# Two padded tail keys taken out of the probability-times-value products of a cross-attention and state-space kernel

## The chip, the cores and the metric

The kernel runs on one core of one Trainium2 chip. The metric is the device time of one execution in microseconds (us), as the median of several runs. PE is TensorE, PEld its weight loads, DVE is VectorE, ACT is ScalarE, POOL is GpSimd and SP is SyncE, whose queue issues DMAs.

## The reference, cut to what matters

```python
x  = layernorm(builder_state, g1, beta1)         # 4096 tokens x 512
bn = layernorm(base_state, g1, beta1)            # 3202 context rows x 512
q, k, v = heads(x Wq), heads(bn Wk), heads(bn Wv)  # 8 heads of 64
attn = softmax(q k^T / sqrt(64))                 # 4096 x 3202 for each head
x  = residual + (attn v) Wo + bo
U  = (layernorm(x, g2, beta2) W_in + b_in) Bmat
s_t = silu(s_{t-1} A^T) + U_t                    # 4096 steps
out = x + s Cmat + mean(program_probs) W_prog + b_prog
```

All of it is in 32-bit floats. 3202 keys are 25 tiles of 128 and two keys more: the 26th tile holds two real keys and 126 padded ones.

## The kernel before

**Stages.** A projection stage goes through 29 groups of 256 rows, 16 of x (giving q) and 13 of the context (giving k and v). For a context group `n = 16 + g` PE does `project_v(n, 0)`, `project_k(n, 0)`, `project_k(n, 1)`, one product for a row maximum, then `project_v(n, 1)`, `project_k(n, 2)`, `project_k(n, 3)` and a second such product. ACT takes the high part of each k chunk out of PSUM (`high_k`, L646), DVE the low part (`low_k`, L911). Then comes attention in 32 units (4 head pairs times 8 blocks of 512 queries), and then a closing stage: output projection, second layernorm, the scan over tokens, the sum.

**A unit of attention.** Unit u goes through 26 key tiles in 13 steps j, two tiles a step. In each step PE does, in this order: one product for a maximum of the unit ahead (L1176, or L1181 for the tail of the keys), the scores of both tiles (a broadcast product of the shift, L1270, and three products, L1278, L1280, L1282, for a high and low split), the second product for a maximum, and `pv` (L1303) for the two tiles of the step before; the `pv` of two tiles shows as x8, four records a tile. So `pv` of tiles 24 and 25 of unit u-1 stands in step 0 of unit u. From unit 1 on, the odd tile's shift isn't a product but is added by DVE (`add_shift`, L995). ACT takes the exponential of each tile into one of six `pt` slots (`exp_tile`, L715, and L712 for tile 25, with a bias that makes the padded keys zero). DVE reduces each product for a maximum (`take_max`, L922 or L925), and the pair of PSUM banks that it frees is the only one: `maxima` waits on PE until all maxima before it are taken (`max_taken`).

**The maxima** of a unit are 26: 24 over 512 keys each (m = 0 to 23) and two over the last 130 keys (m = 24 and 25), which are shorter. The maxima of unit 0 are made in the projection stage, two in each group, and the last four behind it. Those of unit w > 0 are made 4 steps ahead and into unit w-1; unit 0 has 34 of them in its 13 steps, so that some steps have three. In later units m = 24 and 25 fall in step 8. Then `row_max` folds them, PE turns the result with four transposes (`turn_max`, L1190, in step 9) and ACT writes the shift row `sh` (`shift`, L689), which the first scores of the next unit wait for.

**The softmax sum** is taken tile by tile: tiles 1, 5, ..., 21, 24 by accumulating DMAs into `acca` (`send_a`), tiles 3, ..., 19 into `accb` (`send_b`), the other 14, tile 25 among them, by GpSimd into `accp` (`add_tile`, L533). A `pt` slot is free for the exponential six tiles later when its sum and its `pv` are done. `spread_sum` in step 3 adds over partitions, `take_den` (ACT, step 4), `fold_den` (SP), `invert` (DVE, step 6) and `spread_rden` (SP) give a broadcast of 1/sum; GpSimd multiplies O by it in tile 18 (`scale_o`, L569), ACT and GpSimd split the result, and SP stores it (`store_o`).

**The queue of SP** in unit u: wait for the scores of unit u-1, load ql, qh, in units 8 to 11 and 16 to 19 a quarter of the next keys (832 KB), then `fold_den(u-1)`, `spread_rden(u-1)`, `spread_shift(u+1)`, `store_o(u-1)`.

Of the kernel before, what the change touches and what calls it, by code (L numbers as in the profile page):

```python
# [5 lines left out]
F32 = mybir.dt.float32  # L6
# [6 lines left out]
P = 128  # L13
# [28 lines left out]
PAD_SCORE = -2.0 ** 100  # L42
# [6 lines left out]
M_FIRST = NM + 2 * M_LEAD  # L49


def maxima_of(u, j):

    if u == 0:
        first, last = M_FIRST * j // NJ, M_FIRST * (j + 1) // NJ
    else:
        first = M_FIRST + 2 * (NJ * (u - 1) + j)
        last = first + 2
    return [(i // NM + 1, i % NM) for i in range(first, min(last, NM * (UNITS - 1)))]


def turn_step(u):

    return NJ - M_LEAD if u else NM * NJ // M_FIRST + 1

# [6 lines left out]
P_TILES = [t for t in range(NT) if t not in A_TILES + B_TILES]  # L72
# [20 lines left out]
MOD_LO = 96  # L93

# [24 lines left out]
def unit(w):  # L119

    return w % BLOCKS, PAIR_ORDER[w // BLOCKS]

# [21 lines left out]
def build(nc, x, ctx, ctxb, w_qkv_t, w_o_t, w_in, bmat, w_prog_t, a_t, cmat, cols, bo_rows, b_prog, out):  # L144
    es = ExitStack()
    with es:
# [10 lines left out]
        k_scratch = nc.dram_tensor("k_scratch", [2, P, 2, KPAD], F32).ap()  # L157
        m_scratch = nc.dram_tensor("m_scratch", [2, 2, QB], F32).ap()
# [38 lines left out]
        den8 = at("den8", [P, 8], 2560)  # L197
        rden8 = at("rden8", [P, 8], 2568)
# [5 lines left out]
        mxp = at("mxp", [P, QT, HD + 1], RR + 11776)  # L204
        mx_part = at("mx_part", [P, QT, 2, 7], RR + 12040)
        oraw = at("oraw", [P, QB], RR + 12096)
        lnb = at("lnb", [P, 64], RR + 12096)
# [22 lines left out]
        pad = small[:, 31:32]  # L230
# [67 lines left out]
        max_turned = sem("max_turned"); shift_ready = sem("shift_ready")  # L298
# [32 lines left out]
        def _(sp):  # L331
# [21 lines left out]
            def store_k(g):  # L353
                for p in (0, 1):
                    sp.wait_ge(k_ready, FC * g + (p + 1))
                    keys = slice(g * GW, (g + 1) * GW)
                    sp.dma_start(k_scratch[p][:, :, keys], kk[:, p, :, keys].bitcast(F32)).then_inc(k_stored, 16)

            def spread_shift(w):
                sp.wait_ge(shift_ready, w + 1)  # L360
                sp.dma_start(m_scratch[w % 2], sh[w % 2][0:HD + 1:HD, :].bitcast(F32)).then_inc(sh_stored, 16)
                sp.wait_ge(sh_stored, 16 * w)
# [3 lines left out]
            def fold_den(u):  # L366
                sp.wait_ge(den_taken, u + 1)
                for i in range(4):
                    sp.dma_start(den8[32 * i:32 * (i + 1), :],
                                 den_sb[32 * i:32 * i + 1, 0:QB // 2].rearrange("o (p j) -> o p j", j=8)).then_inc(den8_loaded, 16)  # L370

            def spread_rden(u):
                sp.wait_ge(rden_ready, u + 1)
                sp.dma_start(r_scratch[u % 2].rearrange("h (p j) -> (h p) j", j=8), rden8[:, :]).then_inc(rden_stored, 16)
# [25 lines left out]
            for n in range(X_SLOTS, NG):  # L400
# [3 lines left out]
                if n == X_SLOTS + X_G + 1:  # L404
                    for half in (0, 1):
                        sp.wait_ge(q_stored[half], 32 * (X_G // 2))
                    load_qh(0)
                if n - X_SLOTS - 1 >= X_G:
# [3 lines left out]
            sp.wait_ge(proj_done, projected(NG - 1))  # L412
# [3 lines left out]
            store_k(C_G - 1)  # L416

# [15 lines left out]
            for u in range(UNITS):  # L433
# [30 lines left out]
            for d in range(2, X_G):  # L464
                if d >= OG_SLOTS:
# [28 lines left out]
        def _(pool):  # L494
# [5 lines left out]
            nc.gpsimd.memset(mxp[:, :, :], 0.0)  # L500
            nc.gpsimd.memset(pad[:, :], PAD_SCORE)
            nc.gpsimd.memset(ones_row[:, :].bitcast(F32), 0.0).then_inc(ones_set, 1)
            pool.wait_ge(ones_set, 1)
            nc.gpsimd.memset(pad[0:KEYS - (NT - 1) * P, :], 0.0)
# [15 lines left out]
            pool.wait_ge(proj_done, projected(NG - 1))  # L520
# [44 lines left out]

            def scale_o(u):
                pool.wait_ge(rdenb_loaded, 32 * (u + 1))
                pool.wait_ge(o_taken, u + 1)
# [12 lines left out]
            for u in range(UNITS):  # L581
                for t in range(NT):
# [4 lines left out]
                    else:  # L587
                        add_tile(u, t)
                    if t == 18 and u > 0:
# [9 lines left out]
            for d in range(2, X_G):  # L599
                add_bias(d)  # L600
                if d == 10:
# [892 lines left out]
```

## Time and profile before

| what | value |
|---|---|
| median of 3 runs | 2315.91 us (2312.77 to 2317.89) |
| the profiled execution, its own time | 2315.49 us |
| its span, first to last instruction | 2313.7 us |
| mean granted TensorE clock | 0.989 |
| PE, PEld, DVE busy | 2254.5, 1306.4, 1733.4 us |
| ACT, POOL busy | 1110.4, 1583.7 us |
| accumulating DMAs' queue (q0), other queue (q1) | 46.2% and 19.3% of 16 engines |

A row of a group gives the source line, engine, operation, output and input, shapes and count, then busy time and the mean of one. A row of the timeline gives start, length, engine, line and what ended the idle time before it. The ends of matmuls are modelled, so the start of one instruction and the start of the next tell more than the lengths.

### The profile page before, as it was taken

The numbers are of one execution on the slowest core, as the hardware profiler recorded it, in microseconds if no ns is written. First come the engines' busy times: TensorE is split into PE (matmuls) and PEld (weight loads), VectorE is DVE, ScalarE is ACT, GpSimd is POOL, SyncE is SP. The second block draws the span as 40 slices with busy tenths as digits, with TensorE's granted clock in tenths as the row PEclk, the third lists the DMA queues.
The fourth block names the chain that finished last, engine by engine and source line by source line (L and its number), as shares of the span: only waits on it lengthen the run. The fifth ranks groups of instructions, "written<-read, shape, count | busy, mean of one in ns | idle before, by whom it ended". The sixth has DMA issues, their size and how long they took to land.

```text
span 2313.7 us, 36253 instructions
## 1 busy us (share of the span) xinstructions
PE 2254.5 (97%) x14262; PEld 1306.4 (56%) x14262; DVE 1733.4 (75%) x2167; ACT 1110.4 (48%) x1422; POOL 1583.7 (68%) x1039
## 2 busy tenths in 40 slices
PE   8999989999999999999999999999999999999987
PEld 8998854554555544555555455555555555445764
DVE  5765446888888778888888788888888888755865
ACT  3654424445445445444454544544544545453454
POOL 1200026888888888888888888888888888887312
PEclk8999999999999999999999999999999999999998
DMA  6660225677777777777777777677677776787723
GB/s 241 211 193 10 83 64 118 147 160 159 157 160 155 165 167 171 174 158 161 157 159 169 174 174 173 156 166 158 151 158 162 161 160 155 185 186 172 240 100 145
DMA packets 159703, 365.02 MB, mean 158 GB/s; under 512 B 23535, under 2 KB 63087, under 8 KB 158894
## 3 DMA queue, kind: packets, MB, share of 16 engines
q0 software_dynamic: 59904, 218.13, 46.2%
q1 hardware_dynamic: 99630, 144.59, 19.3%
q8 instruction: 112, 1.84, 0.3%
q14 instruction: 57, 0.47, 0.1%
HBM read 95.41 MB, written 49.02 MB: 62 GB/s over the span
## 4 chain that ended last, share of the span: by engine, by line
PE 81%; DMA 5%; POOL 4%; issue 4%; DVE 4%; ACT 1%; POOLq 0%; SPq 0%; DVEq 0%; ACTq 0%
PE ps L1303 28%; PE ps L1176 10%; PE ps L1278 7%; PE ps L1280 7%; PE ps L1282 7%; DMA acca<-pt 5%; PE ps L1140 4%; PE ps L1270 4%; PE ps L1158 3%; PE ps L1148 3%; POOL accp L533 3%; PE ps L1368 2%; PE ps L1121 1%; DVE mx_part L922 1%; PE ps L1425 1%
## 5 line engine op out<-in xcount | busy, mean ns | idle before, releaser
L715 ACT ACTIVATE pt<-ps 128x1024 f32<-128x1024 f32 x800 | 779.3, 1021 | 908.5 <-PE ps L1282 878.2
L922 DVE TENSOR_REDUCE mx_part<-ps 128x2 f32<-128x1024 f32 x768 | 938.0, 1221 | 338.5 <-PE ps L1176 338.4
L533 POOL TENSOR_TENSOR accp<-accp,pt 128x1024 f32<-128x1024 f32 x416 | 1040.5, 2501 | 220.7 <-ACT pt L715 219.0
L1303 PE MATMUL ps<-pt,v 128*64 128x512 f32 x3328 | 805.6, 605 | 0.0
L995 DVE TENSOR_TENSOR ps<-ps,shb 128x1024 f32<-128x1024 f32 x403 | 493.1, 1224 | 52.1 <-PE ps L1282 52.1
L1303 PEld LDWEIGHTS ps<-pt,v 128*64 128x64 f32 x3328 | 201.8, 136 | 344.0 <-issue 335.3
L1176 PE MATMUL ps<-kk,qh 64*128 64x512 f32 x1536 | 349.0, 450 | 10.0 <-DVE mx_part L922 10.0
L1176 PEld LDWEIGHTS ps<-kk,qh 64*128 64x128 f32 x1536 | 143.3, 183 | 355.2 <-DVE mx_part L922 268.6
L1278 PE MATMUL ps<-qh,kk 64*128 64x512 f32 x1664 | 328.8, 391 | 6.9 <-ACT pt L715 6.9
L1280 PE MATMUL ps<-qh,kk 64*128 64x512 f32 x1664 | 328.5, 390 | 0.0
L1282 PE MATMUL ps<-ql,kk 64*128 64x512 f32 x1664 | 328.2, 389 | 0.0
L543 POOL DMA_DIRECT2D acca<-pt x192 | 183.5, 956 | 4.6 <-DMA acca<-pt 2.3
L1278 PEld LDWEIGHTS ps<-qh,kk 64*128 64x128 f32 x1664 | 157.3, 185 | 43.8 <-ACT pt L715 10.4
L1280 PEld LDWEIGHTS ps<-qh,kk 64*128 64x128 f32 x1664 | 157.1, 184 | 35.4
L1282 PEld LDWEIGHTS ps<-ql,kk 64*128 64x128 f32 x1664 | 157.3, 184 | 34.8
L1270 PE MATMUL ps<-sh,ones_row 64*128 64x512 f32 x858 | 173.8, 402 | 1.0 <-ACT pt L715 1.0
L553 POOL DMA_DIRECT2D accb<-pt x128 | 129.6, 1012 | 0.0
L522 POOL MEMSET sh<- 128x512 f32 x2 | 1.0, 530 | 187.2 <-PE ps L1158 187.2
L1368 PE MATMUL ps<-wo_hl,og 128*128 128x512 f32 x384 | 95.5, 404 | 7.0 <-DVE x_first L1038 6.1
L1270 PEld LDWEIGHTS ps<-sh,ones_row 64*128 64x128 f32 x858 | 82.4, 187 | 15.1 <-ACT pt L715 12.0
L1368 PEld LDWEIGHTS ps<-wo_hl,og 128*128 128x128 f32 x384 | 72.6, 193 | 27.4 <-issue 12.7
L578 POOL TENSOR_TENSOR xb<-xb,bo 128x512 f32<-128x512 f32 x32 | 40.7, 1326 | 65.4 <-DMA xb<-x 65.3
(154 smaller groups left out, 1898.3 us busy)
## 6 DMA issues: line engine op xcount, KB each, us to landing
acca<-pt POOLq DMA_DIRECT2D x224, 512.0 KB, 4.9
accb<-pt POOLq DMA_DIRECT2D x160, 512.0 KB, 4.8
q_scratch<-kk SPq DMA_DIRECT2D x32, 512.0 KB, 4.4
acca<-accp POOLq DMA_DIRECT2D x32, 512.0 KB, 4.6
o_scratch<-ost SPq DMA_DIRECT2D x32, 512.0 KB, 3.0
og<-o_scratch SPq DMA_DIRECT2D x32, 512.0 KB, 5.9
shb<-m_scratch SPq DMA_DIRECT2D x31, 512.0 KB, 4.1
xs<-x SPq DMA_DIRECT2D x16, 512.0 KB, 6.4
```

The source lines that it names most:

```text
L533: nc.gpsimd.tensor_tensor(acc[:, :], acc[:, :], pt[n % PT_SLOTS][:, :], ALU.add).then_inc(added_p, 1)
L543: nc.gpsimd.dma_start(acc[:, :], pt[n % PT_SLOTS][:, :], accum_op=ALU.add).then_inc(added_a[u % 2], 16)
L715: nc.scalar.activation(pt[n % PT_SLOTS][:, :], src, ACT.Exp, scale=SCALE).then_inc(exped, 1)
L922: nc.vector.tensor_reduce(mx_part[:, m % QT, :, m // QT], src, AX_X, ALU.max).then_inc(max_taken, 1)
L995: nc.vector.tensor_tensor(ps[:, b:b + 2, :], ps[:, b:b + 2, :], shb[u % 2][:, :, :], ALU.add)\
L1176: ins = mm(ps[:, bank, :], q[r, (m % QT) * P:(m % QT + 1) * P], kk[r, p, 0, a:a + QB], start=True, stop=True)
L1270: ins = mm(ps[:, 2 * (t % 2) + h, :], ones_row[r, :], sh[u % 2][r, :], start=first, stop=not first)
L1278: mm(ps[:, b + h, :], kk[r, p, 0, key], qh[u % 3][r, :], start=first, stop=False)
L1280: mm(ps[:, b + h, :], kk[r, p, 1, key], qh[u % 3][r, :], start=False, stop=False)
L1282: ins = mm(ps[:, b + h, :], kk[r, p, 0, key], ql[u % 2][r, :], start=False, stop=last)
L1303: ins = mm(ps[HD * h:HD * (h + 1), 6, :], v[:, t, f:f + HD], pt[n % PT_SLOTS][:, h * QB:(h + 1) * QB], start=(t == 0), stop=(t == NT - 1))
L1368: ins = mm(ps[:, 2 + t, :], og[:, d % OG_SLOTS, a, k, rows], wo_hl[:, b, k], start=(i == 0), stop=(i == len(PASSES) - 1))
```

## The change

The tail tile's two keys leave `pv`. Their exponentials (two partitions) go to DRAM and come back broadcast over 64 partitions for each head (`tailb`, 512 KB), ACT multiplies each by its v column (`scale_tail`), and GpSimd adds the two products to O (`add_tail`). Tile 25 also leaves GpSimd's sum: its two rows are loaded by DMA beside the folded sum, and DVE adds them (`invert`). The maxima are turned by one transpose of 8 columns; the 8x128 result goes through DRAM into the shift row (`send_shift`). Eight maxima of unit 1 and one of unit 0 move: groups g = 3 to 10 of the context get a third product, for unit 1, group 11 a third one for unit 0, and the last group is written anew with maxima between its k chunks and v last. Within a unit the two short maxima move from step 8 to step 0. Cut to its core:

```diff
+M_EARLY = NM + 2 * M_LEAD
+M_ORDER = [*range(2 * M_LEAD), NM - 2, NM - 1, *range(2 * M_LEAD, NM - 2)]
 def maxima_of(u, j):
+    first = M_EARLY + 2 * (NJ * u + j)
+    return [(i // NM, M_ORDER[i % NM]) for i in range(first, min(first + 2, NM * UNITS))]
-P_TILES = [t for t in range(NT) if t not in A_TILES + B_TILES]
+P_TILES = [t for t in range(NT - 1) if t not in A_TILES + B_TILES]
+def ctx_maxima(g):
+    if g < 2:
+        return []
+    if g == C_G - 1:
+        return [(0, m) for m in range(21, NM)]
+    third = [(1, g - 3)] if 3 <= g < C_G - 2 else [(0, 20)] if g == C_G - 2 else []
+    return [(0, 2 * (g - 2)), (0, 2 * (g - 2) + 1)] + third
...
# SP
+            def send_shift(w):
+                sp.wait_ge(shift_ready, w + 1)
...
+                sp.dma_start(m_scratch[w % 2].rearrange("h (q k) -> (h q) k", k=P), shift_row[:, :].bitcast(F32)).then_inc(sh_stored, 16)
+                sp.wait_ge(sh_stored, 16 * (w + 1))
+                sp.dma_start(sh[w % 2][0:HD + 1:HD, :].bitcast(F32), m_scratch[w % 2]).then_inc(sh_loaded, 16)
+            def send_tail(u):
+                n = NT * u + NT - 1
+                sp.wait_ge(exped, n + 1)
...
+                sp.dma_start(t_scratch[u % 2], pt[n % PT_SLOTS][0:TAIL_KEYS, :]).then_inc(tail_stored, 16)
+                sp.wait_ge(tail_stored, 16 * (u + 1))
+                wait(sp, o_scaled, u)
+                for h in (0, 1):
+                    sp.dma_start(tailb[HD * h:HD * (h + 1), :, :],
+                                 t_scratch[u % 2:u % 2 + 1, :, h * QB:(h + 1) * QB].to_broadcast([HD, TAIL_KEYS, QB]))\
+                        .then_inc(tail_loaded, 16)
+                wait(sp, rden_ready, u)
+                sp.dma_start(den8[:, 1:1 + TAIL_KEYS, :], t_scratch[u % 2].rearrange("k (p j) -> p k j", j=8)).then_inc(den8_loaded, 16)
             def spread_rden(u):
+                sp.wait_ge(tail_added, TAIL_KEYS * (u + 1))
...
                 if u > 0:
+                    send_tail(u - 1)
                     fold_den(u - 1)
                     spread_rden(u - 1)
                 if u + 1 < UNITS:
+                    send_shift(u + 1)
                     spread_shift(u + 1)
...
             for d in range(2, X_G):
+                if d == 4:
+                    send_tail(UNITS - 1)
# GpSimd
+            def add_tail(u):
+                pool.wait_ge(tail_scaled, u + 1)
+                pool.wait_ge(o_taken, u + 1)
+                for k in range(TAIL_KEYS):
+                    wait(pool, tail_added, TAIL_KEYS * u + k)
+                    nc.gpsimd.tensor_tensor(oraw[:, :], oraw[:, :], tailb[:, k, :], ALU.add).then_inc(tail_added, 1)
...
+                    if t == 10 and u > 0:
+                        add_tail(u - 1)
# ScalarE
+                    if t_ == NT - 1:
+                        act.wait_ge(tail_stored, 16 * (v_ + 1))
...
+                for k in range(TAIL_KEYS):
+                    ins = nc.scalar.activation(tailb[:, k, :], tailb[:, k, :], ACT.Copy, scale=v_tail[:, p, k:k + 1])
+                ins.then_inc(tail_scaled, 1)
...
                     if j == 4 and u > 0:
+                        scale_tail(u - 1)
                         take_den(u - 1)
# VectorE, context groups
+                    early = ctx_maxima(g)
+                    if g < C_G - 1:
+                        for w, m in early[:1]:
+                            take_max(w, m)
+                        for i in range(FC):
+                            low_k(g, i)
+                        for w, m in early[1:]:
+                            take_max(w, m)
+            for i in range(FC):
+                take_max(*ctx_maxima(C_G - 1)[i])
+                low_k(C_G - 1, i)
...
+                nc.vector.tensor_reduce(rden8[:, :], den8[:, :, :].rearrange("p k j -> p j k"), AX_X, ALU.add).then_inc(den_summed, 1)
# TensorE
+            def maxima(w, m):
+                wait(pe, max_taken, nth_max(w, m))
...
+                    if g < C_G - 1:
+                        project_v(n, 0)
+                        project_k(n, 0)
+                        project_k(n, 1)
+                        early_maxima(early[:1])
+                        project_v(n, 1)
+                        early_maxima(early[1:2])
+                        project_k(n, 2)
+                        project_k(n, 3)
+                        early_maxima(early[2:])
+            for i in range(FC):
+                early_maxima(ctx_maxima(C_G - 1)[i:i + 1])
+                project_k(NG - 1, i)
+            early_maxima(ctx_maxima(C_G - 1)[FC:])
+            project_v(NG - 1, 0)
+            turn_max(0)
+            project_v(NG - 1, 1)
...
-                for q in range(QT):
-                    ins = nc.tensor.transpose(ps[0:HD + 1, 7, q * P:(q + 1) * P], mxp[:, q, :], ident[:, :])
+                nc.tensor.transpose(ps[0:2 * QT, turn_bank(w), 0:P], mx_row[:, :, :].rearrange("p h q -> p (h q)"), ident[:, :])\
+                    .then_inc(max_turned, 1)
...
                 n, p = NT * u + t, unit(u)[1]
+                if t == NT - 1:
+                    return
...
+            pe.wait_ge(exped, NT * UNITS)
             pe.wait_ge(wo_lo, FC)
```

`nth_max(w, m)` is the place of a maximum in the order in which all are made. In unit 0's step 0 the scores of both tiles now come ahead of their shifts. Eight DMAs of 128 single elements load the v columns once.

## Rows read from the trace of the kernel before

**Rows 1.** Page, the chain that ended last, by engine.
```profile
PE 81%; DMA 5%; POOL 4%; issue 4%; DVE 4%; ACT 1%; POOLq 0%; SPq 0%; DVEq 0%; ACTq 0%
```
**Rows 2.** Groups by line: names, shapes, count | busy, mean ns | idle before, releasers.
```profile
L533 POOL TENSOR_TENSOR accp<-accp,pt 128x1024 f32<-128x1024 f32 x416 | 1040.5, 2501 | 220.7 <-ACT pt L715 219.0 <-ACT pt L712 0.8
...
L715 ACT ACTIVATE pt<-ps 128x1024 f32<-128x1024 f32 x800 | 779.3, 1021 | 908.5 <-PE ps L1282 878.2 <-DMA acca<-pt 27.5 <-PE ps L1270 1.8
...
L569 POOL TENSOR_TENSOR oraw<-oraw,rdenb 128x512 f32<-128x512 f32 x32 | 40.9, 1278 | 0.0
...
L1190 PE MATMUL ps<-ident,mxp 128*65 128x128 f32 x128 | 21.3, 290 | 1.1 <-DVE mxp L932 1.1
```
**Rows 3.** Timeline, one usual step (unit 12): start, length, engine, line.
```profile
1002.28 0.50 PE L1176 MATMUL ps<-kk,qh 64*128 64x512 f32 x2
...
1002.85 0.40 PE L1278 MATMUL ps<-qh,kk 64*128 64x512 f32 x2
...
1004.55 1.94 PE L1303 MATMUL ps<-pt,v 128*64 128x512 f32 x8
...
1005.10 1.22 DVE L922 TENSOR_REDUCE mx_part<-ps 128x2 f32<-128x1024 f32 x1
...
1006.42 0.50 PE L1176 MATMUL ps<-kk,qh 64*128 64x512 f32 x2
```
**Rows 4.** Timeline, step 8 of a unit, where both maxima are short.
```profile
594.95 0.45 PE L1181 MATMUL ps<-kk,qh 64*128 64x130 f32 x4
...
597.10 1.94 ACT L715 ACTIVATE pt<-ps 128x1024 f32<-128x1024 f32 x2 [2.20 <-PE ps L1282]
...
597.55 0.69 DVE L925 TENSOR_REDUCE mx_part<-ps 128x4 f32<-128x520 f32 x1
...
599.02 0.50 PE L1176 MATMUL ps<-kk,qh 64*128 64x512 f32 x2
```
**Rows 5.** Stretches: one step 9, with the turn; length, busy PE, PEld, DVE, ACT, POOL, PEclk, DMA share.
```profile
488.86:493.77 4.91, 4.91 (x32) 2.50 (x31) 3.59 (x3) 2.42 (x4) 4.02 (x3) 1.00 0.74 139
```
**Rows 6.** Timeline around the end of a context group, last k chunk and second maximum.
```profile
301.83 0.49 PE L1176 MATMUL ps<-kk,qh 64*128 64x512 f32 x2
...
302.44 0.48 DVE L911 SCALAR_TENSOR_TENSOR kk<-ps,small,kk 128x256 fp32r<-128x256 f32 x1 [0.95 <-ACT kk L646]
302.84 1.22 DVE L922 TENSOR_REDUCE mx_part<-ps 128x2 f32<-128x1024 f32 x1
```
**Rows 7.** Timeline of PE, last context group to unit 0; the last two rows are one of its steps.
```profile
302.25 3.06 PE L1148 MATMUL ps<-wkv,n 128*128 128x512 f32 x12
...
325.58 0.63 PE L1278 MATMUL ps<-qh,kk 64*128 64x512 f32 x2
...
336.59 0.50 PE L1176 MATMUL ps<-kk,qh 64*128 64x512 f32 x2
...
340.97 0.50 PE L1176 MATMUL ps<-kk,qh 64*128 64x512 f32 x2
```
**Rows 8.** Timeline of ACT: O taken in step 0 of units 1, 2, 9 and 10.
```profile
400.10 0.60 ACT L720 ACTIVATE oraw<-ps 128x512 f32<-128x512 f32 x1 [0.16 <-PE ps L1303]
...
455.26 0.60 ACT L720 ACTIVATE oraw<-ps 128x512 f32<-128x512 f32 x1 [0.16 <-PE ps L1303]
...
842.14 0.60 ACT L720 ACTIVATE oraw<-ps 128x512 f32<-128x512 f32 x1 [0.17 <-PE ps L1303]
...
899.80 0.60 ACT L720 ACTIVATE oraw<-ps 128x512 f32<-128x512 f32 x1 [0.17 <-PE ps L1303]
```
**Rows 9.** Timeline of SP's queue: a store of the shift, and the load that waits for it.
```profile
1048.86 0.52 SPq L361 DMA_DIRECT2D m_scratch<-sh  x1
1050.46 0.33 SPq L364 DMA_DIRECT2D shb<-m_scratch  x1
```
**Rows 10.** Stretches of the closing stage, PE alone: length, busy, PEclk, DMA share, GB/s.
```profile
2127.00:2128.00 1.00, 0.00 (x0) 0.82 1.15 243
...
2134.00:2135.00 1.00, 1.00 (x5) 0.77 1.00 328
```

More of the change, by code:

```diff
@@ L48 @@
 M_LEAD = 4
-M_FIRST = NM + 2 * M_LEAD
+M_EARLY = NM + 2 * M_LEAD
+M_ORDER = [*range(2 * M_LEAD), NM - 2, NM - 1, *range(2 * M_LEAD, NM - 2)]
 def maxima_of(u, j):
[L54 to L64, printed above, removed]
+    first = M_EARLY + 2 * (NJ * u + j)
+    return [(i // NM, M_ORDER[i % NM]) for i in range(first, min(first + 2, NM * UNITS))]
+TURN_STEP = NJ - M_LEAD
 PAIR_ORDER = [2, 3, 0, 1]
@@ L93, with nth_max @@
 MOD_LO = 96
+def ctx_maxima(g):
[5 more added lines that the diff above has]
+    return [(0, 2 * (g - 2)), (0, 2 * (g - 2) + 1)] + third
+EARLY = [p for g in range(C_G) for p in ctx_maxima(g)]
+def nth_max(w, m):
+    return EARLY.index((w, m)) if (w, m) in EARLY else NM * w + M_ORDER.index(m)
 def wait(eng, sem, value):
@@ L121, in unit, with max_bank, turn_bank @@
     return w % BLOCKS, PAIR_ORDER[w // BLOCKS]
+def max_bank(w, m):
+    return 5 if (w, m) in EARLY else 4
+def turn_bank(w):
+    return 7 if w else 0
 def k_slot(w):
@@ L416, in _ @@
             store_k(C_G - 1)
+            sp.wait_ge(ones_set, 3)
+            send_shift(0)
+            sp.wait_ge(v_ready, GT * C_G)
+            sp.dma_start(v_scratch, v[0:TAIL_KEYS, NT - 1, :]).then_inc(v_tail_stored, 16)
+            sp.wait_ge(v_tail_stored, 16)
+            for k in range(TAIL_KEYS):
+                for p in range(PAIRS):
+                    sp.dma_start(v_tail[:, p, k:k + 1], v_scratch[k, p * P:(p + 1) * P].rearrange("(p o) -> p o", o=1)).then_inc(v_tail_loaded, 16)
             def store_o(u):
@@ L979, in _ @@
                     g = n - X_G
[L980 to L986 removed]
+                    early = ctx_maxima(g)
[9 more added lines that the diff above has]
+                low_k(C_G - 1, i)
+            take_max(*ctx_maxima(C_G - 1)[FC])
             row_max(0)
@@ L1183, in maxima, with early_maxima @@
                 ins.then_inc(max_done, 1)
+            def early_maxima(pairs):
+                for w, m in pairs:
+                    pe.wait_ge(k_ready, FC * (C_G - 1 if m >= NM - 2 else 2 * (m // QT) + 1) + 1)
+                    maxima(w, m)
             def turn_max(w):
@@ L1329, in _ @@
                     todo = maxima_of(u, j)
+                    if u == 0 and j == 0:
+                        for t in (0, 1):
+                            open_tile(u, t)
+                            scores(u, t, True, False)
                     for w, m in todo[:1]:
-                        maxima(w, m, m)
-                    if added(u, 2 * j + 1):
+                        maxima(w, m)
+                    if u == 0 and j == 0:
+                        for t in (0, 1):
+                            shift_scores(u, t, False)
+                    elif added(u, 2 * j + 1):
                         open_tile(u, 2 * j)
@@ L1336, in _ @@
                         scores(u, 2 * j + 1, True, True)
+                        scores(u, 2 * j, False, True)
                     else:
                         score_tile(u, 2 * j)
-                    for w, m in todo[1:-1]:
-                        maxima(w, m, m)
-                    if added(u, 2 * j + 1):
-                        scores(u, 2 * j, False, True)
-                    else:
                         score_tile(u, 2 * j + 1)
-                    if ahead and j == turn_step(u):
+                    if ahead and j == TURN_STEP:
                         turn_max(u + 1)
-                    for w, m in todo[max(1, len(todo) - 1):]:
-                        maxima(w, m, m)
+                    for w, m in todo[1:]:
+                        maxima(w, m)
                     if j > 0:
```

223 lines of the change are left out of this document (112 added, 111 removed).

## The prediction, made before the kernel was run

> **What bounds the kernel.** I read the chain that ended last first: PE holds 81% of it [rows 1]. So PE's order is the clock of the kernel, and what leaves PE is worth something only where nothing else is then late. The timeline of a usual step of a unit shows how narrow that is. PE starts a step at 1002.28 and the next at 1006.42, 4.14 us, without a gap, and the `pv` of two tiles takes the last 1.87 of it (1004.55 to 1006.42), 0.94 a tile [rows 3]. But the next step opens with a product for a maximum, which needs the last reduction to be done: that one ends at 1005.10 + 1.22 = 1006.32, only 0.10 before PE comes [rows 3]. DVE's own loop (two reductions, one added shift and the hand-over) is thus some 4.1 us as well. Taking `pv` out of an ordinary step would give 0.1 us at most. That is why the place of the two short maxima matters: with both short, the last reduction ends at 597.55 + 0.69 = 598.24, 3.29 after the step began at 594.95, and PE, which needed 4.07, had 0.8 to spare [rows 4].
>
> GpSimd and ACT are no bound on average: GpSimd waited 220 us for exponentials, ACT 878 us for scores, and 27.5 us for the accumulating DMAs that free its slots [rows 2]. Those last are few long waits, which I come back to.
>
> **The sum, against the profiled execution's 2315.5 us** (the median of the runs is 0.4 us above it, so I carry the result over unchanged).
>
> *Tail out of `pv`, units 1 to 30.* The tile leaves step 0, and the short maxima come there from step 8. PE alone would need 4.07 − 0.94 = 3.13 us for the new step 0. DVE allows the next maximum at 3.29 + 0.05 = 3.34 (0.05 for the hand-over is my estimate, half of the 0.10 seen above), so DVE ends last. Then ACT: its two exponentials of a step end at 597.10 + 1.94 = 599.04, 4.09 into the step [rows 4], while PE wants the second PSUM pair for the odd tile 0.57 into the next step (1002.28 to 1002.85 [rows 3]), which would be at 3.91. With the hand-over PE waits 0.23. Step 8 gets the long maxima and takes 4.14. Before: 4.14 + 4.07 = 8.21; after: 3.34 + 0.23 + 4.14 = 7.71. Saved: 0.50 a unit, 15.0 us in 30 units. From both sides: 0 (if DVE's or ACT's hand-over is worse) to 0.94, 28 us. I take the loop as worked out, since all its parts are rows. Unit 31 makes no maxima and there ACT is late, so nothing.
>
> *One transpose for four.* The step with the turn takes 4.91 us [rows 5], 0.77 more than a usual one; the four transposes are 21.3 / 32 = 0.67 of it [rows 2], 0.17 each. Three less, part of it pipelined: 0.45 us (bounds 0.3 and 0.5). The product for the maximum behind it comes earlier, and DVE isn't late there, as the step is still longer than its 4.1. 30 units: 13.5 us. What it costs is a trip through DRAM: two DMAs, each some 1.6 us from issue to the wait's end (1048.86 to 1050.46 [rows 9]), from step 9 on, with three steps of 4.1 us to spare. Hidden.
>
> *Unit 0.* From its first scores (325.58) to O's copy in step 0 of unit 1 (400.10 [rows 7, 8]) are 74.5 us, less that step and 0.1, 70.3 for 13 steps with 34 maxima. A step with two of them, no added shift, takes 340.97 − 336.59 = 4.38 [rows 7]. After: 12 such, a first step without `pv` (4.38 − 1.87 and 0.4 of wait between its two maxima, 2.9), 0.3 for the turn: 55.8. Saved: 14.5 us (10 to 16).
>
> *The third maximum in context groups 3 to 11.* This is where I expect the cost. On PE it stands behind the last k chunk, and it may start only when the second one is taken. DVE takes the second only after all four `low_k`. Today PE ends the last chunk at 301.8; DVE's `low_k` runs at 302.44, the reduction at 302.84 to 304.06 [rows 6]. So the third product can't start at 301.83 but at 304.1: PE stands still for 2.28 us, and the product itself takes 0.42 (301.83 to 302.25 [rows 6, 7]). 9 × 2.70 = 24.3 us. From below 9 × 0.42 = 3.8 if there is no wait. The stage has no cover for it, PE goes through it without gaps.
>
> *The last group.* From its start (302.25) to the first scores (325.58) are 23.3 us [rows 7], 11 of them nearly empty behind the projection. After: five maxima between four k chunks, DVE in a chain (products at about 0, 1.8, 4.1, 6.0, 7.8 us after a first wait of 1.4), then v, turn and v in 6.3, and 0.8 until ACT has the last v: 16.3 us. The shift's trip through DRAM (3.2 us by [rows 9], perhaps 6 with the q loads ahead of it in the queue) lies beside the second v, ACT's copy and the scores of two tiles, now ahead of their shift. Saved: 7.0 us (3 to 9).
>
> *The tail's own path.* In a unit ACT does two more passes over 128x512, which it has room for in step 4. GpSimd loses one sum of 2.5 us and gets two additions of 1.28 [rows 2], an even trade, late by 2.6 in tile 10, where it is soon waiting for exponentials again. SP gets a write, a wait and three loads at the head of its queue; `fold_den` is behind them, but it waits for `take_den` in step 4 anyway. `take_den` comes 1.2 us later, `invert` is 0.2 longer; covered. What isn't: 512 KB more of broadcast at the start of a unit, where the DMA of tile 24 must land before the exponential of tile 4. In unit 9, one that loads keys, that wait already makes the unit 899.80 − 842.14 = 57.66 us instead of 455.26 − 400.10 = 55.16 [rows 8]. With step 0 shorter by 0.6 these eight units lose about 0.4 each more: 3 us (0 to 10).
>
> *Closing stage.* The last `pv` is 0.9 shorter. `send_tail` of the last unit holds SP for some 4 us ahead of loads: 0 to 5 us, I take 2.
>
> Gains 15.0 + 13.5 + 14.5 + 7.0 + 0.9 = 50.9; costs 24.3 + 3 + 2 = 29.3. Net 21.6: **2294 us**.
>
> **Rivals.**
> *A, the third maximum is hidden.* DVE isn't full in the projection stage, and if the second maximum were taken ahead of the last `low_k`, only 0.42 would remain: 20.5 us less, 2273. Against it: the written order of DVE. Chance 0.14.
> *B, the units don't shorten by the tail.* If DVE's hand-over or ACT's is worse than worked out, step 0 stays near 4.1: 15 us more, 2309. Chance 0.09.
> *C, slower: slot waits in every unit.* The place is ACT's exponential of tiles 4 and 5 in each unit, behind the landing of tile 24's DMA and of the tail's write. Unit 9 shows the price, 2.5 us [rows 8]. It decides from 21.6 / 31 = 0.7 us a unit on; with half of unit 9's price, 1.3, in all 31 units, less the 3 counted, 37 us more: 2331. For it: SP's queue carries ql, qh and then the tail exactly there. Against: ordinary units show no such wait, all of the 27.5 us [rows 2] fall in a third of the units. Chance 0.10.
> *D, PE's clock falls in the projection stage.* In the closing stage PE stood idle from 2124, the granted clock fell in the slice from 2127 (0.82), and it was back in that from 2134 (0.77) [rows 10]: some 6.5 us at 1.2 instead of 2.4 GHz, 3.3 us lost. If each of the nine new gaps did that: 30 us more, 2324. Against: the gaps are 2.3 us, that one was near 4 before the clock fell. Chance 0.05. The Trainium skill, page "TensorE: Matmul & The Clock Gate", Part 1, says that the throttled clock is the default and activity releases it; by that rule gaps where there were none speak against this change. The trace agrees that an idle engine loses the clock, and doesn't show it for a gap this short.
>
> **How the numbers follow.** My forecast keeps 0.62. About 0.2% (4.6 us) is what a measurement of this kernel can tell from no change. Forecast, A and B lie below that limit, C and D above it; with some spread of B and of the forecast to the limit: faster 0.83, same 0.05, slower 0.12. The range takes the bounds of the units' gain (13 us on one side, 15 on the other) with those of the slots and the closing stage, and reaches to A: 2270 to 2318; C, D and a sliver of the best case stay outside.
>
> **What would show it.** The third product of a context group follows a gap near 2.3 us released by a DVE reduction, and PE's stage is about 24 us longer up to the last group. O's copies follow each other at 55.16 − 0.95 = 54.2 us. The step with the short maxima takes 3.3 us and the next one 4.4, with a wait for ACT. Unit 0's O is taken some 56 + 3.5 us after the first scores. If O's copies stand at 53.8 or less, my bound by DVE is wrong; if they stand above 55, it is B or C, told apart by ACT's waits for `acca`; if the gaps in the context groups are missing, it is A; if half-clock slices stand there, D.

## The result, and the profile after

The changed kernel takes **2340.88 us** (median of 4 runs, 2337.73 to 2342.58) against 2316.9 us for the kernel before beside it: ratio 1.0108, 95% interval 1.0094 to 1.0123. It is 24 us slower, where 2294 us and "faster" had been forecast. The profiled execution took 2339.84 us, its span is 2338.0 us, 24.3 us over the span before.

I cut both spans at the same events: the first score of unit 0, the first copy of O by ACT, the last copy of O, the end.

| stretch | before | after | difference | forecast |
|---|---|---|---|---|
| start to first score (projection) | 325.6 | 354.5 | +28.9 | +17.3 |
| first score to first O (unit 0) | 74.5 | 60.8 | −13.7 | −14.5 |
| first O to last O (31 units) | 1712.7 | 1718.2 | +5.5 | −25.5 |
| last O to end (closing stage) | 200.9 | 204.6 | +3.7 | +1.1 |

Two stretches hold the failure: the projection lost 11.6 us more than I had allowed, and the units lost 5.5 where they should have gained 25.5. First the page of the changed kernel: the busy times of the engines (span's share, instructions), the chain that ended last, by engine, and one group by line (times, mean ns, idle before it and its releasers):

```profile
PE 2243.9 (96%) x14038; PEld 1290.2 (55%) x14038; DVE 1734.6 (74%) x2199; ACT 1131.2 (48%) x1486; POOL 1592.1 (68%) x1068
...
PE 81%; DMA 7%; DVE 4%; issue 3%; ACT 2%; POOL 2%; SPq 0%; DVEq 0%; POOLq 0%; ACTq 0%
...
L1014 DVE TENSOR_REDUCE mx_part<-ps 128x2 f32<-128x1024 f32 x768 | 937.5, 1221 | 319.9 <-PE ps L1278 319.8
L595 POOL TENSOR_TENSOR accp<-accp,pt 128x1024 f32<-128x1024 f32 x384 | 984.3, 2563 | 118.6 <-ACT pt L796 112.6
```

Beside [rows 1] PE's share of the chain is what it was, and the DMA's has gone from 5% to 7%. GpSimd's long sum runs 32 times less than in [rows 2], as intended.

**The projection.** PE's timeline, for three of the context groups:

```profile
197.05 0.80 PE L1278 MATMUL ps<-kk,qx 64*128 64x512 f32 x2 [2.26 <-issue]
...
214.93 0.50 PE L1278 MATMUL ps<-kk,qx 64*128 64x512 f32 x2 [2.31 <-DVE mx_part L1014]
215.36 1.10 PE L1222 MATMUL ps<-ident,xs 128*128 128x128 f32 x8
...
231.28 0.80 PE L1278 MATMUL ps<-kk,qx 64*128 64x512 f32 x2 [2.31 <-DVE mx_part L1014]
232.00 1.97 PE L1222 MATMUL ps<-ident,xs 128*128 128x128 f32 x8
```

The third product is there, with the gap that [rows 6] had led me to: 2.31 us before it, released by a reduction on DVE (the first of the nine is 2.26 long, and the view names no releaser for it). But the same two matmuls take 0.50 us behind one gap and 0.80 behind the next, and the eight transposes after them 1.10 and 1.97. The groups are alternately 214.93 − 197.05 = 17.88 and 231.28 − 214.93 = 16.35 us long. The stretches around the gap that ends at 197.05 (length, busy time of PE, PEld, DVE, ACT, POOL, granted clock, DMA share, GB/s), and the whole stage in the last line:

```profile
194.00:197.00 3.00, 0.79 (x7) 0.59 (x5) 2.00 (x3) 0.47 (x1) 0.00 (x0) 1.00 0.00 0
197.00:199.00 2.00, 1.95 (x8) 1.54 (x9) 1.11 (x1) 0.01 (x1) 0.00 (x0) 0.52 0.00 0
199.00:202.00 3.00, 3.00 (x13) 2.55 (x12) 2.39 (x5) 2.59 (x4) 0.00 (x0) 0.75 0.00 0
202.00:206.00 4.00, 4.00 (x30) 3.59 (x29) 1.48 (x3) 1.26 (x3) 0.00 (x0) 1.00 0.00 0
170.00:300.00 130.00, 113.90 (x674) 95.19 (x672) 67.78 (x149) 43.50 (x78) 0.00 (x0) 0.96 0.13 42
```

The granted clock is full while PE is idle, falls just as PE resumes (a mean of 0.52 over the next 2 us, that is 1.2 instead of 2.4 GHz), and is back within some 3.5 us. This happens behind five of the nine gaps (197, 231, 265, 300, 334), in strict alternation in this trace. The alternation isn't fixed: in the traces of experiments 3 and 7, whose projection stage has the same nine gaps, the clock falls behind the first two and then behind the fourth, sixth and eighth.

**The units.** Timelines of ACT, copies of O in step 0 of units 1, 2, 9, 10, 30, 31 and behind unit 31, so that each pair spans one unit (1, 9 and 30; the last pair unit 31); they answer to [rows 8]:

```profile
415.24 0.60 ACT L801 ACTIVATE oraw<-ps 128x512 f32<-128x512 f32 x1
...
469.66 0.60 ACT L801 ACTIVATE oraw<-ps 128x512 f32<-128x512 f32 x1
...
851.38 0.60 ACT L801 ACTIVATE oraw<-ps 128x512 f32<-128x512 f32 x1
...
911.27 0.61 ACT L801 ACTIVATE oraw<-ps 128x512 f32<-128x512 f32 x1
...
2015.65 0.60 ACT L801 ACTIVATE oraw<-ps 128x512 f32<-128x512 f32 x1
...
2076.24 0.60 ACT L801 ACTIVATE oraw<-ps 128x512 f32<-128x512 f32 x1
...
2133.44 0.60 ACT L801 ACTIVATE oraw<-ps 128x512 f32<-128x512 f32 x1 [0.82 <-PE ps L1413]
```

An ordinary unit takes 469.66 − 415.24 = 54.42 us, 0.74 less than before: 21 units are such, 15.5 us gained. But unit 9 takes 59.89 us, and so it goes in all that load something large. The eight that load keys (units 8 to 11 and 16 to 19) stand at 55.32, 59.89, 58.57, 56.90, 56.84, 56.06, 55.40, 58.68, and unit 30, which loads the output weights, at 60.59. Over 54.42 that is 28.5 us; unit 31 is 3.9 us longer than before (57.20 for 53.32).

### The profile page after: what moved, and what is told of

It is laid out like the page before. It is cut to its first block, busy times and chain, and to the rows that moved or that the text cites. A ratio compares the mean times of both kernels' runs of the same rounds, so it can differ in the third digit from the quotient of the medians.

```text
span 2338.0 us, 36251 instructions
## 1 busy us (share of the span) xinstructions
PE 2243.9 (96%) x14038; PEld 1290.2 (55%) x14038; DVE 1734.6 (74%) x2199; ACT 1131.2 (48%) x1486; POOL 1592.1 (68%) x1068
## 4 chain that ended last, share of the span: by engine, by line
PE 81%; DMA 7%; DVE 4%; issue 3%; ACT 2%; POOL 2%; SPq 0%; DVEq 0%; POOLq 0%; ACTq 0%
PE ps L1413 26%; PE ps L1278 10%; PE ps L1390 7%; PE ps L1394 7%; PE ps L1392 7%; DMA acca<-pt 7%; PE ps L1241 4%; PE ps L1382 4%; PE ps L1259 3%; PE ps L1249 3%; PE ps L1481 3%; POOL accp L595 2%; PE ps L1222 1%; ACT pt L796 1%; DVE ps L1094 1%
## 5 line engine op out<-in xcount | busy, mean ns | idle before, releaser
L595 POOL TENSOR_TENSOR accp<-accp,pt 128x1024 f32<-128x1024 f32 x384 | 984.3, 2563 | 118.6 <-ACT pt L796 112.6
L1413 PE MATMUL ps<-pt,v 128*64 128x512 f32 x3200 | 782.3, 608 | 0.0
L1413 PEld LDWEIGHTS ps<-pt,v 128*64 128x64 f32 x3200 | 193.8, 136 | 335.0 <-issue 325.8
L605 POOL DMA_DIRECT2D acca<-pt x192 | 193.5, 1008 | 12.7 <-DMA acca<-pt 11.3
L615 POOL DMA_DIRECT2D accb<-pt x128 | 143.1, 1118 | 0.0
L626 POOL DMA_DIRECT2D acca<-accp x32 | 28.3, 885 | 140.9 <-DMA acca<-pt 104.4
```

Source lines behind the costliest of these rows:

```text
L595: nc.gpsimd.tensor_tensor(acc[:, :], acc[:, :], pt[n % PT_SLOTS][:, :], ALU.add).then_inc(added_p, 1)
L605: nc.gpsimd.dma_start(acc[:, :], pt[n % PT_SLOTS][:, :], accum_op=ALU.add).then_inc(added_a[u % 2], 16)
L1413: ins = mm(ps[HD * h:HD * (h + 1), 6, :], v[:, t, f:f + HD], pt[n % PT_SLOTS][:, h * QB:(h + 1) * QB], start=(t == 0), stop=(t == NT - 2))
```

## The experiments

Three theories stood for the loss. **T1**: 28.9 us of the projection come from the gap alone, which the order of DVE's program makes, and the clock that goes with it. **T2**: the loss in nine units comes from where the tail's store stands on SP's queue, behind the large loads. **T3** (rival of T2): the 512 KB broadcast that each unit now carries makes the slot waits, wherever it stands. A slot wait is ACT's wait for a `pt` slot, ended by an accumulating DMA into `acca`.

The kernel before took 2316.9 us beside the changed kernel, and 2315.04 (experiments 1 to 4), 2314.61 (5 to 8) and 2315.41 us (9 and 10) beside the others, so differences in us to the changed kernel carry some 2 us of that drift.

### 1. DVE's order undone: T1

```diff
-                        for i in range(FC):
+                        for i in (0, 1):
                             low_k(g, i)
-                        for w, m in early[1:]:
+                        for w, m in early[1:2]:
+                            take_max(w, m)
+                        for i in (2, 3):
+                            low_k(g, i)
+                        for w, m in early[2:]:
                             take_max(w, m)
```

> The changed kernel, but in the context groups VectorE takes the second maximum ahead of the last two low parts of k, as TensorE makes it. Theory 1 (the third product waits for the second reduction, which stands behind the last low part, and every second such gap also costs half-clock work): the gaps of 2.3 us ahead of the third product and the half-clock slices go, 9 products of 0.42 us stay. The stage gives back about 29 of the 33 us that it lost; 2312 us. Rival (a third product a group costs that by itself, whatever VectorE's order): within 5 us of the changed kernel.

Measured: 2312.0 us, ratio to before 0.9986 (0.9969 to 1.0003); 28.9 us less than the changed kernel. The first O is copied at 387.32 instead of 415.24, 27.9 us earlier. The stage, in the same columns as above:

```profile
170.00:300.00 130.00, 130.00 (x804) 109.23 (x804) 77.13 (x163) 52.11 (x94) 0.00 (x0) 1.00 0.15 49
```

No idle time on PE, and the clock full. The ninth third product, and the first scores:

```profile
307.61 0.49 PE L1282 MATMUL ps<-kk,qh 64*128 64x512 f32 x2
...
326.55 0.50 PE L1394 MATMUL ps<-qh,kk 64*128 64x512 f32 x2 [0.73 <-issue]
```

The context groups are now all 13.96 us long, for 13.35 before the change (second maxima at 288.48 and 301.83 in that trace): without any gap a third product costs 0.61 us a group. The 31 units take 1718.1 us in all, as in the changed kernel, though single ones differ (unit 8 60.17, unit 9 61.49). So T1 holds for this stage, and the rest of the loss lies elsewhere.

### 2. The tail ahead of the large loads: T2 against T3

```diff
                     load_qh(u + 2)
+                if u > 0:
+                    send_tail(u - 1)
                 pi, part = u // BLOCKS + 1, u % BLOCKS
...
                 if u > 0:
-                    send_tail(u - 1)
                     fold_den(u - 1)
```

> The changed kernel, but the loads of keys, of Wo and of the first O tiles stand behind the tail's write and broadcast in SyncE's queue. Theory 2 (in the units that load keys the tail's write waits in the queue behind 832 KB, the broadcast then starts together with the sums' DMAs, and ScalarE waits for their slots): the tail's write lands some 4 us after its issue instead of 9, the ten units that are longer than 54.4 us lose about 15 of their 28 us; 2326 us. Rival (the bytes collide in whatever order they come): within 4 us of the changed kernel, and the waits for acca stay near 49 us.

Measured: 2318.7 us, ratio 1.0011 (0.9999 to 1.0024), 22.2 us less than the changed kernel, more than expected. The nine units fall to 55.09, 55.60, 55.25, 55.02, 55.06, 55.82, 55.76, 55.19 and 56.79. Read SP's queue at the start of unit 10 of the changed kernel (58.57 us long, 55.25 with the order changed), and behind it an ordinary unit of it:

```profile
907.74 0.58 SPq L435 DMA_DIRECT2D kk<-k_scratch  x1
908.43 0.39 SPq L412 DMA_DIRECT2D t_scratch<-pt  x1
917.62 1.27 SPq L416 DMA_DIRECT2D tailb<-t_scratch  x2
...
1132.10 0.26 SPq L412 DMA_DIRECT2D t_scratch<-pt  x1
1135.44 1.48 SPq L416 DMA_DIRECT2D tailb<-t_scratch  x2
```

Line 412 stores the tail's 8 KB, line 416 waits until they have landed and then broadcasts them. In an ordinary unit this takes 1135.44 − 1132.10 = 3.3 us; behind the load of 832 KB of keys, 917.62 − 908.43 = 9.2 us. The Trainium skill, page "DMA: Bandwidth & Descriptors", section "Queues, rings and completion order", says that each DMA engine takes the descriptors of one ring in their order. The trace agrees: the small store lands about when the load does, whose time to landing in this unit is 9.9 us. The broadcast then starts at the moment at which GpSimd sends the finished sum and the next unit's first tile. GpSimd's timeline in that stretch of the changed kernel:

```profile
908.17 0.83 POOL L605 DMA_DIRECT2D acca<-pt  x1
...
917.44 0.90 POOL L626 DMA_DIRECT2D acca<-accp  x1 [6.03 <-DMA acca<-pt]
...
919.00 0.88 POOL L602 DMA_DIRECT2D acca<-pt  x1
```

The chain that ended last, in the same stretch (start, length, what was waited for or done):

```profile
908.17 8.73 DMA acca<-pt
...
919.00 6.83 DMA acca<-pt
```

And ACT's timeline behind it:

```profile
925.94 1.02 ACT L796 ACTIVATE pt<-ps 128x1024 f32<-128x1024 f32 x1 [3.48 <-DMA acca<-pt]
```

The accumulating DMA sent at 908.17 (tile 24 of unit 9) needs 8.73 us beside the key load, GpSimd stands 6.03 us behind it, so the DMA of tile 1, which must free a slot for tile 7, is sent only at 919.00, and takes 6.83 beside the broadcast. ACT waits 3.48 us, and PE's scores behind it. With the order changed, SP's queue in the same unit:

```profile
903.00 0.26 SPq L412 DMA_DIRECT2D t_scratch<-pt  x1
905.93 1.49 SPq L416 DMA_DIRECT2D tailb<-t_scratch  x2
...
908.12 0.55 SPq L435 DMA_DIRECT2D kk<-k_scratch  x1
```

The chain there:

```profile
903.37 6.70 DMA acca<-pt
...
912.17 7.08 DMA acca<-pt
```

ACT's timeline there:

```profile
919.36 1.02 ACT L797 ACTIVATE pt<-ps 128x1024 f32<-128x1024 f32 x1 [1.73 <-DMA acca<-pt]
```

The tail's store lands in 2.9 us, the first long DMA takes 6.70 instead of 8.73, and ACT's wait is halved. Over the whole kernel, the waits of the changed kernel (who waits, releaser, us, times, longest):

```profile
POOL acca L626 <- DMA acca<-pt: 104.4, 25, 8.3
ACT pt L796 <- DMA acca<-pt: 48.9, 15, 5.1
```

The same waits with the order changed:

```profile
POOL acca L627 <- DMA acca<-pt: 73.7, 25, 4.6
...
ACT pt L797 <- DMA acca<-pt: 23.9, 11, 4.7
```

T2 holds for most of the 28 us: the nine units give back 18.7 of the 28.5. No byte was taken away in this run. But it moved two things at once: the tail's store and broadcast come earlier, and the key load itself is issued 4.75 us behind tile 24's DMA (903.37 and 908.12) where it was 0.43 ahead of it (907.74 and 908.17). That the first DMA takes 6.70 instead of 8.73 us can be the work of either, and no run separates them. Experiment 3 says that the early key load alone isn't the 28 us: there it stands where the change has it, with no tail beside it, and the eight units are 7.4 us over that kernel's ordinary ones, just as here.

### 3. The tail back in `pv` and in GpSimd's sum, all else as changed

Tile 25 also has its exponential over all 128 partitions again, and the v columns aren't loaded.

```diff
-P_TILES = [t for t in range(NT - 1) if t not in A_TILES + B_TILES]
+P_TILES = [t for t in range(NT) if t not in A_TILES + B_TILES]
...
-                if t == NT - 1:
-                    return
...
-                    send_tail(u - 1)
...
-                    if t == 10 and u > 0:
-                        add_tail(u - 1)
...
-                        scale_tail(u - 1)
```

> The changed kernel with the tail tile back in the value products and in GpSimd's sum, no tail through DRAM; one transpose, the new places of the maxima and the new projection stage stay. Theory: a usual unit gets 0.5 us longer (54.9), the extra time of the long units falls from 28 to about 5 and unit 31 loses 4 less, so 12 us faster than the changed kernel: 2329 us, the tail's move is a net loss. Rival (the tail's move pays, the long units are long because all units are shorter): about 15 us slower, 2356 us.

Measured: 2324.17 us, ratio 1.0028 (1.0013 to 1.0043), 16.7 us **less** than the changed kernel. An ordinary unit takes 54.79 us: the tail's move as such was worth 0.37 us in such a unit. The key-loading ones stand at 55.60, 56.33, 56.67, 55.38, 55.63, 55.80, 55.56, 54.79, the last two at 54.46 and 52.89. As the change has it, the move costs more in ten units than it gains in the rest. The closing stage keeps its 204.7 us from the last O on, so what it lost is not the tail's.

### 4. The short maxima back in step 8

```diff
-M_ORDER = [*range(2 * M_LEAD), NM - 2, NM - 1, *range(2 * M_LEAD, NM - 2)]
+M_ORDER = [*range(NM)]
```

> The changed kernel with the two short maxima back in step 8 of each unit. Theory 3 (VectorE's loop of 4.1 us bounds a step with two long maxima): step 0 takes 4.1 us although TensorE has 0.94 less in it, a usual unit takes 54.9 instead of 54.4 us, 15 us slower in all: 2356 us. Rival (TensorE alone sets the step): the place of the short maxima doesn't matter, step 0 takes 3.2 us and step 8 4.1; within 3 us of the changed kernel.

Measured: 2347.61 us, ratio 1.0134 (1.0104 to 1.0165), 6.7 us more than the changed kernel: the right sign, half the size. The intervals of the two ratios overlap; the length of the units, below, is the surer evidence. PE's timeline of a step 0 and the next step in the changed kernel:

```profile
1131.58 0.44 PE L1283 MATMUL ps<-kk,qh 64*128 64x130 f32 x4
...
1134.99 0.49 PE L1278 MATMUL ps<-kk,qh 64*128 64x512 f32 x2
1135.33 0.40 PE L1382 MATMUL ps<-sh,ones_row 64*128 64x512 f32 x2
1135.72 0.51 PE L1390 MATMUL ps<-qh,kk 64*128 64x512 f32 x2
...
1139.41 0.50 PE L1278 MATMUL ps<-kk,qh 64*128 64x512 f32 x2
```

The same step with the short maxima back in step 8:

```profile
1136.46 0.50 PE L1278 MATMUL ps<-kk,qh 64*128 64x512 f32 x2
...
1138.74 1.08 PE L1413 MATMUL ps<-pt,v 128*64 128x512 f32 x4
1140.54 0.50 PE L1278 MATMUL ps<-kk,qh 64*128 64x512 f32 x2 [0.72 <-DVE mx_part L1014]
```

With long maxima in it the step lasts 1140.54 − 1136.46 = 4.08 us, the last 0.72 of it a wait for DVE's reduction, though PE has one `pv` tile less. That is the bound of the prediction, seen directly: taking one tile's `pv` out of a step whose maxima are long gives next to nothing (4.08 us for the usual 4.14). The unit is 54.76, 0.34 longer; the next step begins without the small wait for ACT that the changed kernel has, which returns a part.

### 5. Both orders: experiments 1 and 2 together

> Both repairs together: VectorE's second maximum ahead of the last low parts of k, and the loads of keys, Wo and O behind the tail's write in SyncE's queue. Theories 1 and 2 are about different stages and add: 2341 - 29 - 22 = 2290 us, faster than both kernels. Rival (they share a cost, the units only move): 2305 us or more.

Measured: 2288.2 us (2287.27 to 2296.25), ratio 0.9899 (0.9881 to 0.9917). **Faster than both kernels**, 52.7 us under the changed one; the two single effects sum to 28.9 + 22.2 = 51.1, so within the 2 us of drift they add. The key-loading units lie between 54.36 and 55.60, the last two at 56.88 and 56.20.

### 6. Experiments 1 and 3 together

> The tail back in the value products as in the third experiment, with VectorE's order repaired as in the first. Theory 1 predicts the same 28 us as there: 2324 - 28 = 2296 us. Beside the run with both repairs this gives what the tail's move is worth when it doesn't stand behind the loads: units shorter by 0.35 us, 11 us, less what its waits and the last two units give back, so 3 to 8 us.

Measured: 2294.69 us, ratio 0.9913 (0.9900 to 0.9927). Against experiment 5 this prices the tail's move when it is placed well: 6.5 us gained by the medians. The intervals of the two ratios overlap, so the total is uncertain; the units show the gain more surely (1696.3 us for all 31 against 1703.7). Per ordinary unit it is 54.81 − 54.42 = 0.39; the last two units, 54.03 and 53.15 here, give 5.9 of that back.

### 7 and 8. The broadcast's bytes doubled: T3

A second broadcast of the same two rows, 512 KB more per unit, into a DRAM tensor that nothing reads; in 7 on the changed kernel, in 8 on experiment 5. Both runs have this edit:

```diff
                 wait(sp, rden_ready, u)
+                for h in (0, 1):
+                    sp.dma_start(d_scratch[u % 2, h], t_scratch[u % 2:u % 2 + 1, :, h * QB:(h + 1) * QB].to_broadcast([HD, TAIL_KEYS, QB]))\
+                        .then_inc(dup_loaded, 16)
```

> The changed kernel with the tail's 512 KB broadcast issued a second time in each unit (into DRAM), right behind the first. If bytes at the start of a unit are what ScalarE's slot waits are made of, a second dose of 512 KB costs as much again, 15 us or more, in ordinary units too. If only the place in the queue counts (theory 2), ordinary units stay at 54.4 us and the whole is within 8 us.

> The same second dose in the kernel with both repairs. Theory 2 (the order counts, the engines have room): within 8 us of that kernel, ordinary units at 54.4 us. Rival (bytes count): 15 us or more above it.

Measured: 7 took 2351.24 us, ratio 1.0174 (1.0151 to 1.0196), 10.4 over the changed kernel; 8 took 2303.37 us, ratio 0.9956 (0.9941 to 0.9972), 15.2 over experiment 5. Ordinary units don't see the bytes at all: 54.39 and 54.42 us. Those that load keys do: in 8 they stand at 55.28, 56.72, 58.27, 55.29, 54.65, 58.16, 56.61, 55.23, where 5 had 55 or so, 9.3 us more in all. Not every unit with a large load does: unit 30, which loads the output weights, takes 54.52 in 8 for 56.88 in 5, and 60.43 in 7 for 60.59. (The traced execution of 8 is the shortest of its four, 8.4 us over that of 5, where the medians differ by 15.2; so the trace accounts for about half of the price.) So neither pure theory holds: bytes count, but only in units that load keys as well. T2's "order alone" is too strong, and T3 fails for 21 of 31 units. The second copy goes to DRAM where `tailb` goes to SBUF, so its 15 us is no exact price of the first.

### 9. A shorter gap: what does the clock depend on?

DVE takes the second maximum ahead of the last `low_k` only, which leaves a gap of 0.87 us instead of 2.31. T1's refinement says that a gap this short keeps the clock; its rival, that any repeated gap costs it.

```diff
-                        for i in (0, 1):
+                        for i in (0, 1, 2):
                             low_k(g, i)
...
-                        for i in (2, 3):
-                            low_k(g, i)
+                        low_k(g, 3)
```

(The lines removed are those of experiment 1.)

> The changed kernel, VectorE's second maximum taken ahead of the last low part of k only. By the rows the gap ahead of the third product shrinks from 2.3 to about 0.9 us, 9 x 1.4 = 13 us. If the clock falls because of the length of the gap, the half-clock slices go as well, and the granted clock between 170 and 300 us is 1.00: 21 us faster than the changed kernel, 2320 us. If any gap there brings the clock down (rival), it is 13 us, 2328 us, and the half-clock slices stay.

Measured: 2321.02 us, ratio 1.0031 (1.0018 to 1.0044). PE's timeline at one of the gaps:

```profile
211.76 0.49 PE L1281 MATMUL ps<-kk,qx 64*128 64x512 f32 x2 [0.87 <-DVE mx_part L1014]
```

The stage, in the columns of the stretches above:

```profile
170.00:300.00 130.00, 123.94 (x762) 103.68 (x761) 73.00 (x159) 49.67 (x89) 0.00 (x0) 1.00 0.14 45
```

The clock stays at 1.00 and every group is alike. 9.0 us over experiment 1 for nine gaps of 0.87 (7.8 us): the gap costs its own length, and hardly more. The rival is refuted. The clock next falls at 319.3, in the last group, where a gap of 1.41 us (ended at 318.06) follows that of 0.87 (ended at 316.15): the single gap's length is not all that decides.

### 10. Experiment 5 with the broadcast held back until tile 6

Meant to take the broadcast out of the slots' critical stretch.

```diff
                 sp.wait_ge(tail_stored, 16 * (u + 1))
+                if u < UNITS - 1:
+                    sp.wait_ge(exped, NT * (u + 1) + 7)
```

> The kernel with both repairs, and the tail's broadcast held back until tile 6 of the unit has its exponential, so that it can't meet the DMAs of tiles 24, 1 and the sum. If the broadcast's bytes are what is left of the slot waits (21 us in ten units), about 5 of the 9 us that the long units still have come back: 2283 us. If what is left is the keys' load itself (theory; the kernel before has it too, 4.8 us in these units), nothing changes: 2288 us.

Measured: 2315.53 us, ratio 0.9999 (0.9989 to 1.001): 27.3 us over experiment 5, so both expectations missed. Whom ACT waited for (us, times, longest) shows a cause:

```profile
ACT tailb L812 <- DMA tailb<-t_scratch: 53.6, 28, 3.2
```

ACT's timeline in one unit:

```profile
959.01 1.33 ACT L812 ACTIVATE tailb<-tailb,v_tail 128x512 f32<-128x512 f32 x2 [1.46 <-DMA tailb<-t_scratch]
```

`scale_tail` stands in ACT's program in step 4, and now waits there for the broadcast in nearly every unit (28 times), with the exponentials queued behind it. The 31 units take 21.7 us more than in experiment 5, most of the 27.3. I moved the transfer and forgot its reader. Whether the remaining slot waits would go with the broadcast out of the way stays open.

## Why the prediction was wrong, and where it was right

Two terms of the sum failed: the slot waits, put at 3 us and some 24, and the third maximum in nine groups, put at 24.3 and about 32. Much of the rest came out as worked out.

**The third maximum in nine groups: 24.3 us forecast, about 32 measured.** The gap is the one worked out, 2.28 against 2.31. What failed is the sentence that set rival D aside ("that one was near 4 before the clock fell"): a gap of 2.31 us loses the clock behind every second one. Before, the ninth of these groups ended at 302.25 [rows 7]; now its third product starts at 333.85, at half clock, and ends 0.80 later, at 334.65: 32.4 us. The four groups before it that begin at half clock take 4 × (17.88 − 16.35) = 6.1 of that. The groups at full clock are 16.35 us long for 13.35 before, 3.00 a group where the sum had 2.70; most of that difference is the product, 0.42 in the sum and 0.61 in experiment 1. (Nine times 3.00, 6.1 and 0.3 for the ninth product are 33.4; the first maximum of the stage starts 1.0 earlier than before.) D was thus half true: half as often, and 1.5 us a time where it had 3.3. The Trainium skill, page "TensorE: Matmul & The Clock Gate", Part 1, section on HAM oscillation, tells of a kernel in which a recurring wait makes each pass start at the low clock; here the trace shows it for every second pass.

The kernel before held a warning that I didn't read. PE's timeline in its last context group:

```profile
316.67 0.49 PE L1176 MATMUL ps<-kk,qh 64*128 64x512 f32 x2 [1.79 <-DVE mx_part L922]
318.49 0.75 PE L1176 MATMUL ps<-kk,qh 64*128 64x512 f32 x2 [1.32 <-DVE mx_part L922]
```

The stretch behind it, in the columns used above:

```profile
318.60:328.60 10.00, 6.65 (x32) 4.70 (x34) 4.07 (x5) 1.61 (x2) 0.00 (x0) 0.50 0.19 61
```

Two gaps of 1.79 and 1.32 us within 4 us, no longer one anywhere near, and the clock falls; it stays at half for some 10 us, in which more gaps of up to 1.41 us follow. So the prediction's words that the trace "doesn't show it for a gap this short" are wrong.

**Rival A was the better kernel, not this one.** The idea in it ("if the second maximum were taken ahead of the last `low_k`") is the remedy, but its size was off: just that is experiment 9, which leaves 0.87 us of gap. Two `low_k` earlier, experiment 1, the gap is gone and 28.9 us come back.

**The last group: 7.0 us forecast, 3.4 measured** (354.47 − 334.6 = 19.9 us for 23.3 before; I had 16.3). The ninth gap is one of the five, and the clock was only 0.56 from 336 to 341, twelve matmuls taking 2.93 us that take 1.71 after it: 1.2 us, and 0.3 in each of the two products there. At full clock, in experiment 1, the group still takes 326.55 − 308.10 = 18.45 us, 2.1 more than I had: 0.83 of it is a wait for ACT's copy of v, which wasn't in my chain, and 0.5 a first wait of 1.88 for 1.4.

**Unit 0: right.** 13.7 us saved for 14.5.

**The ordinary unit: right, 54.42 us for 54.2.** Step 0 takes 3.41 for the 3.34 of the prediction, the next one 4.42 for 4.37 (1131.58 to 1134.99 to 1139.41, above), and experiment 4 shows DVE as the bound. The step with the turn takes 4.57 us for the 4.91 of [rows 5]: 0.34 saved, not 0.45. That and the two steps (0.07 and 0.05 longer) are the missing 0.2 of each unit.

**The slot waits: 3 us forecast, some 24 more than before measured.** This is the step that turned the result. The prediction had the right kind of wait and the right units, and even noted that the tail's store would follow ql and qh on SP's queue, but it priced one wait only, tile 4's exponential behind tile 24's DMA, and that one by the 0.6 us that step 0 became shorter. Counting the exponentials in ACT's timeline gives two places in a unit: tile 4, and tile 7 behind tile 1's DMA, which GpSimd sends only after its own wait for tile 24's. Before, ACT waited 12.4 us at the first and 15.2 at the second; in the changed kernel it is 16.7 and 32.2. So 17 of the 21 us more stand at tile 7, which the sum didn't have. The diff puts `send_tail` behind `load_k`, `load_x2` and the weights; I read past that line and thought of 8 KB as free. It takes 9.2 us instead of 3.3 to land, and that moves a 512 KB broadcast into the sums' DMAs; experiment 2 gave back 18.7 us of the nine units by the order alone. Rival C, "slot waits in every unit", had the kind of wait but not the units: up to 5.5 us in the eight that load keys, 6.2 in unit 30, none in 21. Unit 31, put at nothing, is 3.9 longer; its wait at tile 7 is 4.43 us where it was 1.81.

**The closing stage: +1.1 net forecast, +3.7 measured.** It is 204.7 without the tail (experiment 3) and 204.9 in experiment 1, so `send_tail`, to which I had given 2 us, isn't shown as the cause. Nor is any other edit: with the program of this stage unchanged the traces give 204.6 (changed kernel), 206.6 (experiment 2) and 201.9 (5), and without the tail 204.7 (3) and 199.5 (6). The 2.6 us off lie within that scatter, and the cause stays open.

Together: 11.6 in the projection, 0.8 in unit 0, 31 in the units and 2.6 in the closing stage are the 46 us between −21.6 and +24.3. The 31 are 20.7 of slot waits beyond the 3 (28.5, less 4.8 that such units had over an ordinary one before, less 3), 3.9 of unit 31, and 0.22 in each of 30 units.

## What to carry to other kernels

A small DMA whose landing someone waits for belongs ahead of the large loads of its queue; here that order was worth 22 us, with no byte saved. When work is added to an engine whose order is written out, look at where its input is released on the other engine's program: moving one reduction ahead of two low parts of k gave 29 us. And when a transfer is delayed on purpose, move its reader too.

## What the runs showed of the hardware that I had not expected

Nine gaps of 2.3 us, 16.35 or 17.88 us apart, with PE busy between them: the granted clock falls to half behind five of them, for some 3.5 us each; with gaps of 0.87 us in their place it stays full up to the last group. And two gaps of 1.79 and 1.32 us close together, in the kernel before, were followed by 10 us at half clock. An 8 KB store on SP's queue lands after 9.2 us behind an 832 KB load and after 3.3 without one. And 512 KB more of traffic per unit changed nothing in 21 units (54.42 us for 54.40), but added up to some 3 us (58.27 for 55.14) to a unit in which 832 KB were loaded as well: in this kernel the DMA engines' mean busy share of 0.7 to 0.8 didn't tell where bytes cost time.
